# A recurrent mixer with routed experts on one core: row-tiled projections regrouped, buffers and queue work moved, the last triangular inverse divided between two engines

## What is computed

```python
xx = shifted(x) - x;  mix = x + xx*time_maa_x
lo = tanh(mix @ maa_w1.T) -> 4 groups @ maa_w2
xrg, xwa, xk, xv = x + xx*(lo + time_maa)
r = xrg@Wr.T; k = xk@Wk.T; v = xv@Wv.T; g = tanh(xrg@gate_w1.T)@gate_w2
w = -softplus(-(time_decay + tanh(xwa@decay_w1.T)@decay_w2)) - 0.5
kk = k + tanh(xk@kkk_w1.T)@kkk_w2;  kk = kk / norm_per_head(kk)
a, ma, mk = sigmoid(bias + low-rank products)
k = k*(ma + a*(1-ma)) * exp(w*mk);  b = -kk*a
for t: s = s*exp(-exp(w)) + (s@kk) b^T + v k^T;  y = s@r   # per head
y = groupnorm(y)*ln_w + ln_b + sum(r*k*faaaa)*v
x1 = layernorm(x + (y*g)@Wo.T)
e = argmax(x1 @ centroids.T)      # one of 8 experts per token
out = layernorm(x1 + x1 + W2[e] relu(W1[e] LN_e(x1) + b1[e]) + b2[e])
```

## Time and profile before

| | us |
|---|---|
| median of 3 runs (lowest, highest) | 1072.9 (1069.43, 1076.72) |
| the profiled execution: device time | 1076.19 |
| its span, first to last instruction | 1074.1 |
| bodies of the recurrent part, within the span | about 0 to 738 |
| expert part | about 750 to 1074 |

### The profile page before, as it was taken

One profiled execution on the slowest core, in us unless ns is written; L12 is line 12 of the kernel. 1 busy time (PEld: TensorE's weight loads), 2 busy tenths in 40 slices (PEclk: granted clock), 3 DMA queues, 4 the chain that ended last, 5 costly groups with the idle time before them and its releaser, 6 DMA issues.

```text
span 1074.1 us, 42156 instructions
## 1 busy us (share of the span) xinstructions
PE 980.1 (91%) x16652; PEld 801.8 (75%) x16653; DVE 768.0 (71%) x1793; ACT 519.9 (48%) x1081; POOL 613.1 (57%) x1135
## 2 busy tenths in 40 slices
PE   8898989999999989999999998679899999999995
PEld 5676777777777767777777776557899898989894
DVE  5766788889879778887688885266476666666663
ACT  4474576677677576676476783221122121212120
POOL 1088786788886787785867876810133333333321
PEclk9997999999999999998799998689999999999998
DMA  5113225225324225224143133746545445544430
GB/s 121 40 21 81 71 33 110 65 51 111 77 47 101 70 44 111 72 42 107 17 101 87 28 91 85 206 115 232 217 163 176 161 174 162 176 158 170 158 119 4
DMA packets 208894, 112.14 MB, mean 104 GB/s; under 512 B 172508, under 2 KB 192224, under 8 KB 208352
## 3 DMA queue, kind: packets, MB, share of 16 engines
q1 hardware_dynamic: 202352, 100.92, 35.0%
q0 software_dynamic: 3744, 8.40, 2.3%
q10 hardware_dynamic: 2640, 0.54, 0.3%
HBM read 85.57 MB, written 26.08 MB: 104 GB/s over the span
## 4 chain that ended last, share of the span: by engine, by line
PE 61%; DVE 14%; issue 8%; POOL 6%; DMA 5%; ACT 4%; DVEq 1%; SPq 1%; ACTq 0%; POOLq 0%
PE bank L576 16%; PE bank L970 12%; PE bank L983 9%; PE bank L662 6%; PE ry L983 4%; PE bank L718 3%; POOL arena L1914 3%; POOL arena L1911 3%; DVE bank L1389 2%; PE ry L692 2%; PE bank L594 1%; PE bank L622 1%; PE bank L950 1%; PE ry L698 1%; PE bank L740 1%
## 5 line engine op out<-in xcount | busy, mean ns | idle before, releaser
L576 PE MATMUL bank<-arena 128*128 128x256 f32 (+2 forms) x992 | 280.9, 422 | 22.4 <-DVE arena L1434 9.5
L1914 POOL TENSOR_TENSOR arena<-arena 128x30 f32<-128x30 f32 (+14 forms) x480 | 261.6, 545 | 37.6
L1911 POOL TENSOR_TENSOR arena<-arena 128x30 f32<-128x30 f32 (+14 forms) x480 | 250.5, 522 | 36.4
L576 PEld LDWEIGHTS bank<-arena 128*128 128x128 f32 x992 | 178.5, 203 | 67.9 <-issue 31.5
L970 PEld LDWEIGHTS bank<-arena 128*128 128x128 f32 x1248 | 146.8, 194 | 5.8 <-issue 3.0
L970 PE MATMUL bank<-arena 128*128 128x128 f32 x1248 | 147.5, 277 | 3.1 <-DVE arena L1820 2.5
L1498 DVE TENSOR_TENSOR arena<-bank,arena 128x512 f32<-128x512 f32 x128 | 79.5, 684 | 53.1 <-PE bank L662 53.1
L1302 ACT ACTIVATE arena<-arena 128x1 f32<-128x1 f32 x39 | 11.5, 294 | 178.6 <-DVE arena L1774 178.6
L983 PE MATMUL bank<-arena 128*128 x416 | 96.4, 385 | 0.1
L1945 POOL COPY arena<-arena 128x1 int32 (+1 forms) x39 | 7.1, 183 | 146.4 <-DVE arena L1838 146.4
L983 PEld LDWEIGHTS bank<-arena 128*128 128x128 f32 x416 | 76.9, 190 | 14.5 <-issue 4.9
(11 more groups left out here) (173 smaller groups left out, 1757.7 us busy)
## 6 DMA issues: line engine op xcount, KB each, us to landing
arena<-in_W SPq DMA_DIRECT2D x47, 1024.0 KB, 5.1
scr_n<-arena SPq DMA_DIRECT2D x64, 128.0 KB, 3.0
arena<-scr_n SPq DMA_DIRECT2D x16, 512.0 KB, 3.7
scr_u<-arena SPq DMA_DIRECT2D x16, 512.0 KB, 4.5
arena<-scr_u SPq DMA_DIRECT2D x62, 128.0 KB, 2.9
arena<-in_xTp SPq DMA_DIRECT2D x32, 132.0 KB, 4.0
arena<-in_x SPq DMA_DIRECT2D x64, 64.0 KB, 2.7
scr_x<-arena SPq DMA_DIRECT2D x64, 64.0 KB, 1.8
```

The costliest lines, as they stand in the source:

```text
L576: mm = pe.matmul(ring.tile(m, name)[0:rows, to], lhsT, rhs, start=(i == 0), stop=(i == len(terms) - 1))
L1911: inv_ok.inc(f"m{s}", TT(t, U[:, 0:s, s:s + 1].broadcast_to(shape), U[:, s:s + 1, s + 1:TB].broadcast_to(shape), ALU.mult))
L1914: inv_ok.inc(f"a{s}", TT(U[:, 0:s, s + 1:TB], U[:, 0:s, s + 1:TB], t, ALU.add))
```

## The change

It does the following:

- Projections in two waves: z, a and kk together on row groups 0:32, 64:96, 96:128, then the second half of z (32:64) with ma and mk. z is added up in its bank over both waves, the second of which waits for the first (`half_decay`). kk is added by PE onto k in k's bank; `sum_kk` goes from DVE, and ACT copies kk from the bank (`keep_kk`) and squares it from there.
- PE's order: the projection of k ahead of `gates`. ACT's order: a first, then z, sigmoid, kk, its square, the logits, and only then ma, |z|, mk. `keep_keys(n, 1, 1)` goes behind key decay and growths; values are masked from the SBUF copy of v, one step later.
- Banks: norms into z's bank 1, router logits into bank 0 ahead of the output projection, and xa, bk11, v0 moved.
- 512-column matmuls of norms, centre and variance in two of 256.
- DVE: token statistics from in front of the key exponent to behind the masks (while there is a block n+1); r's decayed read behind the bonus product.
- The inverse is stored to DRAM by POOL, straight after it is done; SP only loads the heads, then the tokens. For block 14 the heads are loaded at the end of SP's body 14.
- The last inverse (block 15) is divided: POOL does columns 0 to 24, DVE columns 24 to 32 in PSUM, in three portions between its other work, with a copy of the coefficients by ACT.
- All W2 loads wait for the last heads and are issued in body 16.

The diff, cut to its core:

```diff
+        CUT = 24
+        coefs = view(at_zt, CUT * CUT).rearrange("p (r c) -> p r c", r=CUT)
+        right = banks[2][:, 0:TB * (TB - CUT)].rearrange("p (r c) -> p r c", r=TB)
...
-        proj = Stage(sem("proj"), [(1, "k z0 z1 sg a0 a1 ma0 ma1 abs sq sab mk0 mk1 ln lnss inv W ek iW0 iW1 v "
+        proj = Stage(sem("proj"), [(1, "k a0 a1 z0 z1 sg kk sq ma0 ma1 abs sab mk0 mk1 ln lnss inv W ek iW0 iW1 v "
...
-        ring = Ring(banks, [(0, "bk00@5"), (1, "h@2"), (-2, "g@4"), (1, "k@3"), (0, "bk01@2"), (1, "z@1 a@5 kk@3 ma@4 mk@2"),
-                            (-3, "logit@3"), (-2, "wo@0"), (1, "ss@0"), (-1, "xa@1 xb@3"), (1, "r@4"),
-                            (0, "bk11@5"), (1, "v@2"), (0, "bk10@5 v0@1 v1@3"),
+        ring = Ring(banks, [(0, "bk00@5"), (1, "h@2"), (1, "k@3"), (-2, "g@4"), (0, "bk01@2"), (1, "a@5 kk@3"),
+                            (1, "z@1 ma@4 mk@2"), (-3, "logit@0"), (-2, "wo@0"), (1, "ss@1"), (-1, "xa@5 xb@3"), (1, "r@4"),
+                            (0, "bk11@0"), (1, "v@2"), (0, "bk10@5 v0@0 v1@3"),
...
             def scores_to_pairs(m):
...
                              nd.rearrange("g k f e (h s) t -> (g k f e h) (s t)", h=2)).then_inc(n_in, 16)
                 if m == last:
+                    heads_from_inverse(last - 1)
...
             def body(n):
-                if has(n - 1):
-                    inverse_to_heads(n - 1)
+                if has(n - 1) and n != last:
+                    heads_from_inverse(n - 1)
...
-                if n == last:
+                if n == last + 1:
+                    sp.wait_ge(u_in, NBLK * 64)
                     load_experts(slice(0, 4))
...
             def decay_a_kk(m):
                 hid_act.wait(pe, m, "decay", "copy", "kkk")
+                for name in ("z", "a", "kk"):
+                    ring.wait_empty(pe, m, name)
+                for h, to in both:
+                    mm_z = pe.matmul(ring.tile(m, "z")[:, to], w_out[0:32, 2, hs(h)], hid[0:32, :], start=(h == 0), stop=False,
+                                     skip_group_check=True)
+                    mm_a = pe.matmul(ring.tile(m, "a")[:, to], w_out[64:96, 0, hs(h)], hid[64:96, :], start=True, stop=True)
+                    mm_kk = pe.matmul(ring.tile(m, "kk")[:, to], w_out[96:128, 0, hs(h)], kkh[96:128, :], start=False, stop=True,
+                                      skip_group_check=True)
+                mm_z.then_inc(half_decay, 1)
...
+            def decay_ma_mk(m):
+                pe.wait_ge(half_decay, m + 1)
+                for name in ("ma", "mk"):
+                    ring.wait_empty(pe, m, name)
+                for h, to in both:
+                    mm_z = pe.matmul(ring.tile(m, "z")[:, to], w_out[32:64, 2, hs(h)], hid[32:64, :], start=False, stop=True,
+                                     skip_group_check=True)
+                    mm_ma = pe.matmul(ring.tile(m, "ma")[:, to], w_out[64:96, 1, hs(h)], hid[64:96, :], start=True, stop=True)
+                    mm_mk = pe.matmul(ring.tile(m, "mk")[:, to], w_out[96:128, 1, hs(h)], hid[96:128, :], start=True, stop=True)
...
             def norms(m):
                 proj.wait(pe, m, "sq")
-                fill(m, "ss", [(all_cols, [(head_sum, flat(nrm))])])
+                fill(m, "ss", [(to, [(head_sum, nrm[:, h])]) for h, to in both])
...
+            def keep_kk(m):
+                if m:
+                    comb.wait(act, m - 1, "kkn")
+                ring.wait_full(act, m, "kk")
+                proj.inc(m, "kk", A(flat(kk), bank(m, "kk"), ACT.Copy))
...
+                    keep_a(n + 1)
                     keep_z(n + 1)
                     sigma_of_z(n + 1)
-                    keep_a(n + 1)
+                    keep_kk(n + 1)
+                    square_kk(n + 1)
+                if has(n - 3):
+                    keep_logits(n - 3)
+                if has(n + 1):
                     keep_ma(n + 1)
                     abs_of_z(n + 1)
...
-                if has(n - 2):
+                if has(n - 2) and not has(n + 1):
                     token_stats(n - 2)
                 if has(n + 1):
                     key_exponent(n + 1)
+                if n == last:
+                    start_right(last)
+                    invert_right(last, range(TB - 2, 23, -1))
...
+                if n == last:
+                    invert_right(last, range(23, 12, -1))
...
+                if has(n - 2) and has(n + 1):
+                    token_stats(n - 2)
...
+                if n == last:
+                    invert_right(last, range(12, 0, -1))
+                    keep_right(last)
...
+            def store_inverse(m):
+                if m:
+                    pool.wait_ge(u_in, m * 64)
+                if m == last:
+                    last_inv.wait(pool, 0, "a1")
+                    last_inv_dve.wait(pool, 0, "kept")
+                else:
+                    inv_ok.wait(pool, m, "a1")
+                nc.gpsimd.dma_start(ud, Up[m % 2].rearrange("p r c -> p (r c)")).then_inc(u_out, 16)
+
+            for m in range(NBLK - 1):
                 invert(m)
+                store_inverse(m)
+            invert_left(last)
+            store_inverse(last)
```

140 lines of the change are left out of this document (83 added, 57 removed).

## The result

The changed kernel takes 1115.5 us (median of 4 executions, 1110.6 to 1130.8), the kernel before beside it 1071.2 us (1067.4 to 1076.7): ratio 1.039, 95% interval 1.032 to 1.047. It is slower by 4%, and the time lies above the range of the prediction. Ratios here are formed over the fast executions of each kernel alone (those within 1.5% of its fastest), so they can differ a little from the ratio of two medians.

The account below looks back on a forecast made before the run. In a body DVE, PE and ACT meet within 0.1 to 0.7 us; at the end the last inverse is alone on the path. +2.8 (14 periods) + 1.2 (start) − 3.7 (end) = +0.3 on median 1072.9: 1073, range 1054 to 1088.

Parts of the forecast that it names:

- rival two: Slower: the gap the logit copy opens on PE halves the clock in most bodies; +1.0 a body, +14, 1087; chance 0.18.
- The PE gap of 1.6 us: Between router and output projection PE idles some 1.6 us for ACT's logit copy; PE's 0.75 us saving is given back.
- Body +0.2: One loop body: masks and scores 0.5 us later, split matmuls 0.3 less; +0.2 us, over 14 periods +2.8.
- The split matmuls, −0.3 in the sum: On PE in a body: each split 512-column matmul saves 0.05 to 0.2 us, two on the loop's path, 0.3 in all.
- r's decayed read: On DVE, moved behind the bonus product: frees nothing, since the bonus matmul's bank is r's and `freed` needs that read.
- POOL's store: nothing in a body: Inverse stored by POOL: issue at most 1.06 us, only the next inverse waits behind it; no cost in a body.
- Over 3 us: Sign of being wrong: POOL's store of the inverse costs POOL over 3 us.
- The start, +1.2: First two bodies, no solve to hide behind: z 1.2 us later, L1420's 0.60 gone; 2 x 0.6 = +1.2 us.
- The end, −3.7: Divided last inverse: store issued at 698.5 instead of 702.91, −4.4; POOL's issue costs 0.7 more; net −3.7 us.
- Second expert weights, hidden: Late W2 loads arrive behind the solve at about 706, well before 750; hidden unless they meet instruction fetches.
- From the read-out to the end, nothing: Stretch after the last read-out: the change touches nothing behind 750 us, so the sum has no term for it.
- third and fourth rival: Three: W2 loads stall the last read-out 4.70 us, 1078, chance 0.08. Four: DVE's portions held up, 1077, within forecast's 0.47.

## Why the prediction was wrong, point by point

The forecast was 1073, the measured time 1115.5. That it would be slower by over 1% had a chance of 0.20, and even rival two's 1087 was too low by 28. The ratios above, read one on top of the other, divide the loss (each from another group of runs, so each step is good to some 5 us; the store's by medians is 5 to 9):

| the changed kernel built up | ratio to before | worth of the step |
|---|---|---|
| divided inverse and W2 late | 0.994 | −6 us |
| and everything else but GpSimd's store, with the gap shortened and filled | 1.004 | +11 |
| and GpSimd's store | 1.013 | +9 |
| and the gap as it is in the change | 1.039 | +28 |

**"The PE gap of 1.6 us".** The place and size of the gap were right: 1.79 us, ended by ACT's logit copy, in 11 bodies. The step that failed is its price. The sum gave it nothing, since the solve waited for its DMA behind it anyway, and let it touch the clock only in rival two, at +1.0 us in a body and a chance of 0.18. Two things were missed. First, the delay: in the kernel before, such a gap costs 14 us even when it is filled, 1.2 us in a body, so what stands behind the output projection was not covered. Second, the clock: 32 us there, 20 in the changed kernel. Rival two had this mechanism right and its size wrong: it took one slowed piece (the earlier trace rows against the earlier trace rows, 1.5 us) for the price of a body, while stretches of up to 13.7 us followed the gap, and it knew of no delay beside the clock. The full-clock rows behind gaps of 0.3 to 0.7 us in the earlier trace rows say nothing about gaps of 1.8. The Trainium skill, TensorE: Matmul & The Clock Gate, section A second HAM failure mode: psum-queue depth-cycling, describes a kernel that cycles through PSUM banks, whose TensorE idles briefly between groups of matmuls often enough that its clock goes up and down. The traces here agree for the logit gap, a wait for one PSUM bank of 1.79 or 1.91 us. The length of the wait alone doesn't bring it about: behind the 1.5 to 1.85 us for DVE's read of r half clock did not follow within 5 us.

**"Body +0.2".** Even where the clock stays up the term was mis-sized. The periods of the two full-clock bodies after are 41.7 and 40.9 us, of the five before 39.2 to 39.7: about +1.9. The second of them holds the logit gap; the first ends while PE stands in its first such gap, so the gap is not the only cause. In the frame of the prediction (the first wave's start at 254.85) the clean body after has z at 257.26 (forecast 257.15), the logarithm at 263.72 (263.55), DVE's L1440 at 264.39 (264.2), the keeping of the solution at 265.83 (265.56), the output projection at 259.95 (259.8), the scores at 275.46 (275.1, before 274.57). Each was late by 0.1 to 0.4, always in the same direction, and the path to the scores is longer by 0.9 where the sum had 0.5. The split matmuls, −0.3 in the sum, give nothing. The rest of the difference, between the scores and the next body, was not followed in the sum at all: there 0.7 us more go by in the clean body, as much as the idle pieces of PE for which the profile names no cause ("issue") grow. And of r's decayed read the prediction said that moving it frees nothing; it costs, since PE now waits for it (1.24 us at 500.28; before, it waited 0.47 us there, for the bonus product). That edit was not run alone. The counter-check is the 1.0% that separates the filled kernel with SP's store from the one with the divided inverse alone.

**"POOL's store: nothing in a body".** In a body the profiles show little to contradict this; the store costs 5 to 9 us in the run all the same. In the pair of profiles whose half-clock times agree the larger part lies behind the last scan, 1.3 us of it behind the last scatter. Over 3 us was the prediction's own sign of being wrong. That its issue takes 0.58 us on POOL was the row looked for, and it was harmless: the cost isn't on POOL. The whole of it isn't explained. The estimate of 3.2 us for the store, from the Trainium skill, DMA: Bandwidth & Descriptors, section Anatomy of one DMA, is below the 4.1 us that the page of the profile gives as the median to landing; the measurement decides, and neither length explains 5 to 9 us.

**The start, +1.2.** 2.2 us to the first scan and 4.2 to the second (60.7 where it was 56.5), over which the term was meant. With the waves undone the first stands at 20.5 to 21.1, as in the kernels made from before (20.8 to 21.8), and the second at 56.4 to 56.7; with the waves they stand at 23.7 to 24.4 and 60.7 to 61.4. So the whole of it is the waves and ACT's order with them, which in the first bodies no other block's work hides.

**The end, −3.7.** DVE started its part 5.7 us behind the start of the inverse and had done after 28.2 (forecast 30.4), so this went better than expected, while the solve gained 2.65 us. Between store and solve stood PE's own work at half clock. Where the loop is left alone, the part gives 5 us in the run (2 to 10 by its interval) and 3.3 in the profile: the term was right, and it was the only gain of the change. In the changed kernel itself the stretch gave back 1.9 us of the 3.7.

**Second expert weights, hidden.** Right: 0.999.

**From the read-out to the end, nothing.** It takes 4.6 us more: 1.3 behind the last scatter, 1.6 before the first indirect DMA, which swings by 2 us among kernels of one kind, and 1.7 in the expert part between. The last is steady: the kernels made from the changed one take 77.1 to 77.6 us from one indirect DMA to the twentieth behind it, in the middle of the expert part, and those made from before 76.8 to 77.0, though the code of the expert part is the same. Why was not tried.

The third and fourth rival (a stalled fetch behind the weights, DVE's portions held up) did not come: no issue stall over 2.6 us stands at the end, and the portions were done early. That the stall of 4.70 us before 689.77 had to do with fetching, as the prediction calls it, no run shows; with only the loads late, PE's idle pieces of the kind ("issue") are 1.2 us at most there.

## What to carry to other kernels

When a matmul engine is over 90% busy and a PSUM bank is given to a new neighbour, look at who must empty it and how far down in that engine's order that step stands: the wait is paid once as delay and once more, and dearer, if the clock falls behind it. Test a suspected gap from both sides, filled with matmuls that nobody reads in the kernel that has it, and put alone into the kernel that hasn't. And a change of many parts deserves its parts one by one: here one of them was good, three were neutral, and the loss of the others hid the good one.

## What the runs showed of the hardware

- A gap of 1.91 us ahead of the output projection, once in some 45 us, was followed by half clock 11 times of 11; one of 1.79 us there 8 times of 11. Up to 13.7 us of the body then ran at half clock. The length alone doesn't decide: gaps of 1.5 to 1.85 us at another place of the body, in the filled kernel, were not followed by it within 5 us, 7 times of 7, while in the kernel before a stretch began behind a gap of 0.47 us (503.5 us). A length that is safe was not found.
- Useless matmuls in a wait shorten the run: 20 us in one kernel, 32 in another.
- Two f32 matmuls of 256 columns take as long as one of 512: 1.13 and 1.12 us for the norms.
- Storing 512 KB sixteen times through GpSimd and not SyncE costs 5 to 9 us, some 6 of them at the same mean clock, though it lands no later (median 4.1 us from issue, SyncE's before 4.5), and the program ends 1.3 us later behind the same last instruction.
- Three row groups of f32 matmuls run beside each other: 24 instructions in some 2.3 us, where 20 in pairs and singly took 2.96.
